# Transposing a third weight matrix in 32x32 squares on VectorE instead of with TensorE, in a two-layer fp32 kernel with NF4 dequantisation

## What is computed

```python
def layer1(x):                     # x: 1024 tokens x 512
    approx_up, delta = x @ up_w.T, x @ gate_w.T - local_point          # 512 -> 128
    out = approx_up @ local_approx_output.T
    for m in range(1, 7):          # powers of |delta| / m!, signed, cut off at 2.5 for m > 4
        out = out + (dterm(delta, m) * approx_up) @ fuse_weight[:, :, m - 1].T
    return out + (silu(x @ ffn_gate_w.T) * (x @ ffn_up_w.T)) @ ffn_down_w.T   # 512 -> 1248 -> 512

def nf4(w):                        # blocks of 64 elements along a row
    absmax = max(|block|)
    return nearest of 16 codes to (block / absmax) * absmax

def layer2(x):                     # w1, w2: 1376 x 512; w3: 512 x 1376
    h = silu(x @ nf4(w1).T) * (x @ nf4(w2).T)
    return h @ nf4(w3).T

x = layernorm(x + layer1(x)); x = layernorm(x + layer2(x))
```

## Time and profile before

| | us |
|---|---|
| three runs, median | 418.53 |
| lowest, highest | 418.44, 418.89 |
| the profiled execution, its own time | 419.06 |
| its span, first to last instruction | 417.2 |
| TensorE's granted clock over the span | 0.994 of full speed |

### The profile page before, as it was taken

How to read it: one execution, slowest core, us unless ns; L and a number is a source line. 1 busy time by engine, 2 the same in 40 slices (tenths; PEclk the granted TensorE clock), 3 DMA queues, 4 the chain that set the end, 5 groups by cost and what they waited for, 6 DMA issues and landing times.

```text
span 417.2 us, 5429 instructions
## 1 busy us (share of the span) xinstructions
PE 408.3 (98%) x1820; PEld 334.0 (80%) x1820; DVE 314.2 (75%) x371; ACT 263.9 (63%) x356; POOL 291.3 (70%) x230
## 2 busy tenths in 40 slices
PE   8999999999999999999999999999999999999992
PEld 6888888888878888788888888888888878888882
DVE  3629879879887978999969989898999874115025
ACT  5476676686877547557864976879867864332612
POOL 0078998888995499917992668999989984444330
PEclk9999999999999999999999999999999999999997
DMA  8993110000004342003042000000000000000202
GB/s 267 395 409 131 52 38 26 27 25 25 27 25 126 102 147 101 26 0 103 0 176 97 2 0 1 2 0 0 3 0 0 2 0 2 1 2 1 101 2 101
DMA packets 9355, 26.50 MB, mean 64 GB/s; under 512 B 1296, under 2 KB 1552, under 8 KB 8816
## 3 DMA queue, kind: packets, MB, share of 16 engines
q1 hardware_dynamic: 9328, 26.16, 17.8%
HBM read 24.06 MB, written 2.10 MB: 63 GB/s over the span
## 4 chain that ended last, share of the span: by engine, by line
PE 91%; POOL 2%; DVE 2%; DMA 2%; issue 1%; ACT 0%; SPq 0%; POOLq 0%
PE PS L1178 30%; PE PS L1180 30%; PE PS L1179 30%; DMA h<-xT 2%; POOL l_lo L1133 1%; PE PS L1291 1%; PE PS L1281 1%; POOL level L1103 1%; DVE stats L889 1%; DVE R L884 0%; ACT R L659 0%; DVE x_lo L970 0%; ACT x_hi L573 0%; DVE mv L898 0%; SPq L537 0%
## 5 line engine op out<-in xcount | busy, mean ns | idle before, releaser
L1103 POOL TENSOR_SCALAR level<-side 128x1024 f32<-128x1024 int8 (+2 forms) x119 | 130.0, 1092 | 29.3 <-DVE PS L812 12.1
L1178 PE MATMUL PS<-x_hi,w_hi 128*128 128x512 f32 (+1 forms) x352 | 137.6, 391 | 0.2 <-DVE x_lo L970 0.2
L1180 PE MATMUL PS<-x_hi,w_lo 128*128 128x512 f32 (+1 forms) x352 | 137.1, 390 | 0.0
L1179 PE MATMUL PS<-x_lo,w_hi 128*128 128x512 f32 (+1 forms) x352 | 137.0, 389 | 0.0
L812 DVE TENSOR_TENSOR PS<-PS,level 128x1024 f32<-128x1024 f32 (+2 forms) x102 | 120.3, 1179 | 21.5 <-POOL level L1103 16.8
L573 ACT ACTIVATE side<-Q 128x1024 int8<-128x1024 f32 (+1 forms) x77 | 76.5, 1031 | 18.6 <-DVE PS L808 9.7
L1133 POOL TENSOR_TENSOR l_lo<-h,l_hi 128x512 fp32r<-128x512 f32 (+1 forms) x42 | 58.3, 1396 | 38.5 <-ACT l_hi L573 38.0
L1178 PEld LDWEIGHTS PS<-x_hi,w_hi 128*128 128x128 f32 (+1 forms) x352 | 65.2, 185 | 15.0 <-issue 0.6
L1180 PEld LDWEIGHTS PS<-x_hi,w_lo 128*128 128x128 f32 (+1 forms) x352 | 65.2, 185 | 14.9
L1179 PEld LDWEIGHTS PS<-x_lo,w_hi 128*128 128x128 f32 (+1 forms) x352 | 65.2, 185 | 14.5
L1178 PE MATMUL PS<-x_hi,l_hi 128*128 128x512 f32 x144 | 56.7, 394 | 0.0
(11 more groups left out here) (77 smaller groups left out, 500.4 us busy)
## 6 DMA issues: line engine op xcount, KB each, us to landing
Q<-w SPq DMA_DIRECT2D x10, 512.0 KB, 13.8
raw<-w_in SPq DMA_DIRECT2D x9, 512.0 KB, 11.4
raw<-w_out SPq DMA_DIRECT2D x14, 256.0 KB, 2.6
raw<-w SPq DMA_DIRECT2D x2, 1376.0 KB, 8.4
R<-xN SPq DMA_DIRECT2D x2, 1024.0 KB, 5.4
out<-R SPq DMA_DIRECT2D x8, 256.0 KB, 2.0
raw<-w_fuse SPq DMA_DIRECT2D x7, 256.0 KB, 2.5
h<-xT SPq DMA_DIRECT2D x3, 512.0 KB, 7.1
```

What stands on the lines that cost most here:

```text
L1103: g.tensor_scalar(level_of(s), side_of(s), LIMITS[k][1], LIMITS[k][0], ALU.min, ALU.max).then_inc(s_level, 1)
L1178: t_.matmul(dst, a_hi, b_hi, start=start, stop=False)
L1179: t_.matmul(dst, a_hi, b_lo, start=False, stop=False)
L1180: return t_.matmul(dst, a_lo, b_hi, start=False, stop=stop)
```

## The change

w3 is laid out by the host in squares, as w1 and w2 are, so that VectorE can transpose it: `turn_w3(c)`, one transpose of 128x512 out of the unit into bank 4 + c % 2. TensorE's transposes of w3 are gone. The six w3 units are now pairs of chunks (1024 columns; the last one chunk, 96x512, in `Q[:, 0]`, the others in `raw`), each loaded by its own transfer; the first five wait for the last use of their slot of `raw`, the sixth for the first `turn_nf4`. In this layout a block of 64 elements of a row is in two halves of 32, that lie on different partitions. VectorE takes maxima of the halves (`maxima_of_w3`, at steps 68, 70, ..., 78, which are 8.4 to 9.6), ScalarE copies each half's maximum to where the other half lies (`bring_partners`, ten small copies, before step 10.2), VectorE takes the greater and the reciprocals of all units at once (`scales_of_w3`, at step 10.3). `up2`, the place of the up products, moves from `Q[:, 0]` to `Q[:, 1]`, and ScalarE's first copy into it waits for the second `turn_nf4`. The table SHARE is new for all three engines.

```diff
-PAIR = 2 * F2
...
-UNITS = C2 + 2 * W3_PARTS
+ROWS3 = D // SQ
+W3_UNITS = (C2 + 1) // 2
+UNITS = C2 + W3_UNITS
 def unit_width(u):
...
-    return UW if is_last_third(u) else 2 * NARROW * BLOCK
+    return D * min(2, C2 - 2 * (u - C2))
 def w3_unit_of(c):
-    return C2 + 2 * min(W3_PARTS - 1, (2 * c + 2) // NARROW) + 1
+    return C2 + c // 2
...
+W3_MAXIMA = {NB * (C2 - 3) + 4 + 2 * k: k for k in range(W3_UNITS)}
+W3_PARTNERS, W3_SCALES = NB * C2 - 6, NB * C2 - 5
...
 SHARE = {
     "scalar": [
-        0, 0, 0, 4, 2, 2, 1, 0, 3, 0, 2, 0, 0, 2, 1, 3, 0, 1, 3, 0, 4, 2, 0, 3, 3, 0, 4, 2, 0, 2, 5, 0, 3, 0,
+        0, 0, 0, 4, 0, 4, 1, 0, 3, 0, 1, 0, 1, 3, 0, 3, 0, 1, 3, 0, 4, 0, 1, 4, 3, 0, 4, 2, 0, 2, 5, 0, 3, 0,
...
-        up2 = Q[:, 0, :].rearrange("p (i n) -> p i n", i=2)
+        w3_last = Q[:, 0, 0:D]
+        amax3, rcp3 = (Q[:, 0, i:i + C2 * ROWS3] for i in (D, D + C2 * ROWS3))
+        up2 = Q[:, 1, :].rearrange("p (i n) -> p i n", i=2)
...
         def w3_bank(c):
-            return 4 + c % W3_BANKS
+            return XT_BANK + c % 2
...
-            wait_split(sp, len(JOBS) - 1)
-            wait_split(sp, VECTOR_LOW[-1])
-            for q in range(2):
-                sp.dma_start(w3_tile(q), w3[q * P:(q + 1) * P, :]).then_inc(s_w3[q], 16)
+            for k in range(W3_UNITS):
+                u = C2 + k
+                if u < UNITS - 1:
+                    wait_split(sp, max(j for j in range(len(JOBS)) if j % RAW_SLOTS == k))
+                else:
+                    sp.wait_ge(s_turn, 1)
+                sp.dma_start(unit_read(u), (w3[:, k * UW:(k + 1) * UW] if u < UNITS - 1 else w3_end)).then_inc(s_w3[k], 16)
...
+            def bring_partners():
+                act.wait_ge(s_max3, W3_UNITS)
...
+                copy(other[a, :, even], own[b, :, even]).then_inc(s_other, 1)
...
             def draw_line(s):
                 u, k = STEPS[s]
+                if s == W3_PARTNERS:
+                    bring_partners()
...
-                act.wait_ge(s_w3tr, c + 1)
+                act.wait_ge(s_w3turn, c + 1)
                 wait_w3_slot(act, c)
-                copy(w_slot(2, ("w3", c), p)[0].rearrange("p (q j r) -> p q r j", q=2, r=2),
-                     PS[0:p, w3_bank(c), :].rearrange("p (q r j) -> p q r j", q=2, r=2)).then_inc(s_whi4, 1)
+                copy(w_slot(2, ("w3", c), p)[0].rearrange("p (i b) -> p i b", i=SQ),
+                     PS[0:p, w3_bank(c), :].rearrange("p (b i) -> p i b", i=SQ)).then_inc(s_whi4, 1)
...
+            def maxima_of_w3(k):
...
+                v.tensor_reduce(unit_scales(amax3, u), by_block(u, unit_read(u)), AX_X, ALU.max,
+                                apply_absolute_value=True).then_inc(s_max3, 1)
+            def scales_of_w3():
+                dve.wait_ge(s_other, 10)
+                v.tensor_tensor(amax3, amax3, rcp3, ALU.max).then_inc(s_max3_all, 1)
...
+            def turn_w3(c):
+                beside()
+                dve.wait_ge(s_dq, quantised(w3_unit_of(c)))
+                dve.wait_ge(s_wlo4, C2 + max(0, c - 1))
+                v.transpose(PS[0:rows(c, F2), w3_bank(c), :], w3_chunk(c)).then_inc(s_w3turn, 1)
...
                     for c in range(2):
+                        turn_w3(c)
+                    for c in range(2):
                         lo_w3(c)
-            for c in range(2, W3_BANKS):
+                        turn_w3(c + 2)
+            for c in range(2, W3_AHEAD):
                 lo_w3(c)
+                turn_w3(c + 2)
...
-            def transpose_w3(c):
-                m = rows(c, F2)
-                pe.wait_ge(s_dq, quantised(w3_unit_of(c) if w3_bank(c) < 6 else UNITS - 1))
-                pe.wait_ge(s_wlo4, C2 + (c - W3_BANKS + 1 if c >= W3_BANKS else 0))
-                for q in range(2):
-                    for r in range(2):
-                        last = t_.transpose(PS[0:m, w3_bank(c), (2 * q + r) * P:(2 * q + r + 1) * P],
-                                            w3_tile(q)[:, r * F2 + c * P:r * F2 + c * P + m], ident[:])
-                last.then_inc(s_w3tr, 1)
```

More of the change, by code:

```diff
@@ L156, in units_ahead @@
     return [u for u in range(UNITS) if max(0, NB * u - ahead) == s]
-SCALE_GROUPS = [range(0, 1)] + [range(u, u + 2) for u in range(1, UNITS, 2)]
+SCALE_GROUPS = [range(0, 1)] + [range(u, u + 2) for u in range(1, C2, 2)]
+W3_MAXIMA = {NB * (C2 - 3) + 4 + 2 * k: k for k in range(W3_UNITS)}
+W3_PARTNERS, W3_SCALES = NB * C2 - 6, NB * C2 - 5
 def adds(s):
@@ L271, in build @@
         l_hi, l_lo = sb("l_hi", [P, L_SLOTS, HALF], F32R), sb("l_lo", [P, L_SLOTS, HALF], F32R)
-        raw = sb("raw", [P, 2 * PAIR])
+        raw = sb("raw", [P, RAW_SLOTS * 1024])
         Q = sb("Q", [P, C2, UW])
@@ L345, in build @@
         s_q = [sem(f"s_q{i}") for i in range(C2)]
-        s_w3 = [sem(f"s_w3_{q}") for q in range(2)]
+        s_w3 = [sem(f"s_w3_{k}") for k in range(W3_UNITS)]
         s_out = sem("s_out")
@@ L453, in w3_bank, with normalised @@
         def w3_bank(c):
-            return 4 + c % W3_BANKS
-        def unit_count(u):
-            return sum(2 if is_last_third(x) else 1 for x in range(u + 1))
+            return XT_BANK + c % 2
         def scaled(u):
[L463 to L468, removed]
+            return [u in group for group in SCALE_GROUPS].index(True) + 1 if u < C2 else len(SCALE_GROUPS) + 1
+        def normalised(u):
+            return u + 1
+        quantised = normalised
         def unit_read(u):
@@ L472, in unit_read, with w3_chunk, by_block, unit_scales @@
                 return Q[:, u, 0:unit_width(u)]
[L473 to L481, removed]
-            if u < C2:
[L483 to L494, removed]
-        def spread(t, u, b, n):
-            v, p = per_block(t, u, b, n), unit_rows(u)
-            if n == 2 * NARROW:
-                return v.unsqueeze(3).broadcast_to([p, 2, NARROW, BLOCK])
-            return v.unsqueeze(2).broadcast_to([p, n, BLOCK])
+            k = u - C2
+            return (w3_last if u == UNITS - 1 else raw[:, k * UW:(k + 1) * UW])[0:unit_rows(u)]
+        def w3_chunk(c):
+            k = c % 2 * D
+            return unit_read(w3_unit_of(c))[:, k:k + D]
+        def by_block(u, tile):
+            return tile.rearrange("p (b e) -> p b e", e=BLOCK if u < C2 else SQ)
+        def unit_scales(t, u):
+            if u < C2:
+                return t[:, (u + 1) % t.shape[1], 0:unit_width(u) // BLOCK]
+            b = (u - C2) * UW // SQ
+            return t[0:unit_rows(u), b:b + unit_width(u) // SQ]
+        def spread(t, t3, u):
+            v = unit_scales(t if u < C2 else t3, u)
+            p, n = v.shape
+            return v.unsqueeze(2).broadcast_to([p, n, BLOCK if u < C2 else SQ])
         def side_of(s):
@@ L573, in copy @@
                 return nc.scalar.activation(dst, src, ACT.Copy, **kw)
+            def bring_partners():
+                act.wait_ge(s_max3, W3_UNITS)
+                own, other = (t.rearrange("p (c b) -> p c b", b=ROWS3) for t in (amax3, rcp3))
+                even, odd = slice(0, ROWS3, 2), slice(1, ROWS3, 2)
+                a, b, c, d = (slice(i * SQ, (i + 1) * SQ) for i in range(4))
+                full = slice(0, C2 - 1)
+                later = slice(1, C2)
+                copy(other[a, :, even], own[b, :, even]).then_inc(s_other, 1)
+                copy(other[b, :, even], own[a, :, even]).then_inc(s_other, 1)
+                copy(other[c, full, even], own[d, full, even]).then_inc(s_other, 1)
+                copy(other[d, full, even], own[c, full, even]).then_inc(s_other, 1)
+                copy(other[b, :, odd], own[c, :, odd]).then_inc(s_other, 1)
+                copy(other[c, :, odd], own[b, :, odd]).then_inc(s_other, 1)
+                copy(other[d, full, odd], own[a, later, odd]).then_inc(s_other, 1)
+                copy(other[a, later, odd], own[d, full, odd]).then_inc(s_other, 1)
+                copy(other[c, C2 - 1, even], own[a, 0, odd]).then_inc(s_other, 1)
+                copy(other[a, 0, odd], own[c, C2 - 1, even]).then_inc(s_other, 1)
             def draw_line(s):
                 u, k = STEPS[s]
+                if s == W3_PARTNERS:
+                    bring_partners()
                 if k == 0:
                     act.wait_ge(s_nrm, normalised(u))
-                    if is_last_third(u):
-                        act.wait_ge(s_dq, quantised(u - 4))
                 if s >= NR:
@@ L1334, in _ @@
                     transpose_x(TILES + 1)
-                elif (f, half) == (C2 - 1, 0):
-                    for c in range(2):
-                        transpose_w3(c)
-            for c in range(2, W3_BANKS):
-                transpose_w3(c)
             for n in range(PASS_START[2], PASS_START[3] - TAILS[2]):
@@ L1382 @@
     fuse = a(L0_attn_fuse_weight)
+    w3_rows = np.zeros((D, C2 * P), np.float32)
+    w3_rows[:, :F2] = a(L0_ffn_w3)[order]
+    w3_rows = w3_rows.reshape(SQ, ROWS3, C2, P // SQ, SQ)
     arrays = {
@@ L1394 @@
         "w12": by_squares(a(L0_ffn_w1), a(L0_ffn_w2)),
```

(4 more changed lines are left out.)

78 lines of the change are left out of this document (36 added, 42 removed), and 24 rows, old and new, of the table SHARE.

## The result

The changed kernel takes **413.5 us** (median of 4 runs, 413.27 to 413.98) where the kernel before takes 418.61 (4 runs, 418.44 to 418.89): a ratio of 0.9878, interval 0.9866 to 0.9889. Predicted were 413.3 us, in a range of 412.6 to 415.8. The profiled execution took 413.98 us and spans 411.8; before it was 417.2, so 5.4 us less.

A forecast was written before the change was run, and what follows sets the result against it. The prediction took TensorE, busy 98% of the span, as the bound. Saving 0.87 + 0.98 + 7 x 0.48 = 5.2 us, with all added work costed at nothing, gave 418.53 - 5.2 = 413.3 us, range 412.6 to 415.8.

The forecast's parts named there:

- The 5.2 us taken off: TensorE's queue: removing the 44 transposes of w3 saves 0.87 + 0.98 + 7 x 0.48 = 5.2 us.
- 7 x 0.48: First pass over w3: seven jobs with four transposes each, every period 0.48 us shorter without them (3.20 to 2.72).
- The 0.87 and 0.98 us: TensorE's chain: cost of two sets of eight transposes, the 0.98 holding some 0.11 us of waiting for the last dequantised unit.
- Rival 3: No gain: the transposes filled time in which TensorE would wait anyway; 418.5 us, chance 0.03.
- What VectorE got: VectorE's added work: eleven transposes at 0.68 us, 7.5 together; low halves 0.69 each; new maximum and reciprocal under 1 us.
- Rival 2: First w3 pass: PSUM reads at a stride of 32 elements are dear, VectorE becomes the bound; 421 to 426.5 us, chance 0.05.
- Is it hidden: First w3 pass: VectorE's new chain costs nothing, with cover of 2.4 us at chunk 2 and about 7 at chunk 10.
- the last pair's banks: TensorE's first w3 job, third tile: ScalarE frees these banks with a margin of only 0.2 to 0.3 us.
- Place (a): Layer 1, input chunk 7: GpSimd's low half ends at 94.7 against 95.0, margin 0.3 us; no wait, up to 1 us.
- Place (b): Boundary of the layers: two w3 maxima on VectorE between products feeding the normalisation; costs nothing, up to 1 us.
- Place (c): GpSimd's queue of low halves until 168.7, same instructions in another order: nothing, 0.5 us either way.
- Rival 1: The new deal leaks: margins of 0.3 us don't hold, costing 0.7 to 3 us; 414.0 to 416.5 us, chance 0.17.

The follow-up runs named there:

- the doubling: The kernel before with every transpose of w3 done twice on TensorE (88 instead of 44): 423.65 us.
- b_none: The kernel before without any transpose of w3 on TensorE, queues and deal of steps otherwise as before (w3 not transposed, time only): 415.53 us.
- a_in7: The changed kernel with one more level ahead of the low half of input chunk 7 on GpSimd: 414.94 us.
- a_early: The changed kernel with VectorE's last eleven steps (7 of ScalarE's, 6 of GpSimd's) put back, VectorE's all ahead of chunk 0's low half: 426.87 us.
- the tripled kernel: The changed kernel with each of VectorE's eleven transposes of w3 done three times: 424.73 us.

## Why the prediction was right

**The bound.** TensorE without a pause, and every other engine free until late: right. Its busy time fell by 5.1 us (408.3 to 403.2), and the other 0.3 of the 5.4 are small waits.

**The 5.2 us taken off.** The number was right and one part of its reason was not. 7 x 0.48 is what the period shows (3.20 to 2.72), and the doubling confirms it. The 0.87 and 0.98 us for the two sets of eight came back too (1.8 us: the first matmul of w3 is 2.0 us earlier, 0.3 of it from before this stage), but not because the transposes had cost that. b_none shows that with them gone TensorE waits 1.66 us at the same place, for a low half that stood behind the last unit. The step that was incomplete is in "What the change removes", where I took them as cost of their own, with only 0.11 us of waiting in them. The fact stood one part further on ("the last unit was written just as TensorE asked for it"); the conclusion, that these 1.85 us come only if the new deal moves that unit out of the way, was not drawn. It did, and the prediction had laid out the new queue and found no wait in it, so the sum held; but these 1.85 us are right by luck as the price of the transposes, for which they were taken. Rival 3 was right in the small: of the 5.2 us some 1.7 lay beside work that TensorE would have had to wait for.

**What VectorE got.** The transposes take 714 ns each (I took 0.68 us), the low halves with their stride of 32 elements 670 (0.69), ScalarE's split 590 (two w_hi of 128x512), less than the 630 of the earlier trace rows and no more than its plain copies out of PSUM of that width (592). Rival 2's premise, a dear read of PSUM at a stride, is false: here it is free. Its counter-argument held for VectorE alone: before, ScalarE's split wrote every second element and took 628 ns (two w_hi), 0.04 us more than a plain copy. Two small terms were under-sized: the scales of all w3 units take 0.33 + 0.76 + 1.25 = 2.35 us where I said under 1. I had left out the middle one, which sets a floor under the maxima. The reciprocal goes with the count (0.35 us for 32 numbers, 1.25 for 176); why the middle one takes 0.76 is not shown, but the same instruction on 32 numbers took from 0.17 to 1.22 us in this execution. The ten copies take 2.6 us where I said about 2. Both stand some 90 us ahead of their use: GpSimd waited 1.5 us for the reciprocals, TensorE for neither.

**Is it hidden.** Yes. VectorE after, in the stretch that was laid out:

```profile
340.86 0.68 DVE L974 TENSOR_TENSOR w_lo<-PS,w_hi 128x512 fp32r<-128x512 f32 x1
...
346.50 0.69 DVE L974 TENSOR_TENSOR x_lo<-PS,x_hi 128x512 fp32r<-128x512 f32 x1 [0.27 <-ACT x_hi L559]
...
363.38 0.67 DVE L974 TENSOR_TENSOR x_lo<-PS,x_hi 128x512 fp32r<-128x512 f32 x1
364.12 0.69 DVE L974 TENSOR_TENSOR w_lo<-PS,w_hi 96x512 fp32r<-96x512 f32 x1
```

Chunk 2 is ready at 347.2 (predicted near 347.6), chunk 10 at 364.8 (near 365). The cover at chunk 2 is 2.4 us, as said, and at chunk 10 6.6; chunk 9, with 4.6, was passed over. At the last pair's banks the margin of 0.2 to 0.3 us was not there: the third tile's first matmul (345.56) took 0.30 us to the next start instead of 0.23. The two evacuations run from 344.39, just behind the end of the pair's last record, to 345.46. The next job's six matmuls had begun at 344.19 already; I had counted them from that end. The margin for ScalarE's own queue was 1.0 us rather than 0.2.

**Place (a).** GpSimd's low half of chunk 7 after, and ScalarE's evacuation of pair 13, which answer to the earlier trace rows:

```profile
92.29 2.41 POOL L1152 TENSOR_TENSOR w_lo<-raw,w_hi 128x1024 fp32r<-128x1024 f32 x1
```
```profile
95.05 0.60 ACT L642 ACTIVATE h<-PS 128x512 f32<-128x512 f32 x1 [1.18 <-PE PS L1210]
```

It ends at 94.70, the predicted 94.7, and TensorE loses under 0.05 us (the pair's first two matmuls start at 94.85 and 95.11). It took 2.41 us, the shorter of the two times in the earlier trace rows.

**Place (b).** No wait; between 214.2 and 217 TensorE even comes 0.17 us further ahead of the kernel before, and what had held it there is not shown. VectorE reaches the first maximum at 213.75 (predicted 213.9) and its data are there (a transfer of 512 KB landed 3.9 us after its issue, median of five); the last low half of x is there 0.3 us sooner than before:

```profile
213.75 1.18 DVE L805 TENSOR_REDUCE Q<-raw 128x32 f32<-128x1024 f32 x1
...
233.52 1.29 DVE L937 TENSOR_TENSOR x_lo<-PS,x_hi 128x512 fp32r<-128x512 f32 x2 [0.74 <-ACT x_hi L559]
```

**Place (c).** Up to 0.2 us gained rather than nothing: behind the matmul at 168.29 TensorE stood still for 0.35 us before, behind that at 168.38 for 0.19 after. It is inside the 0.5 us allowed.

**Rival 1** (leaks) did not happen, though a_in7 shows that one more step of 1.1 us at (a) would have given it. Its chance of 0.17 was not too high: of three margins called small, that at (a) was, that at the banks was gone by 0.07 us while ScalarE's own was misread, and (b) was put to no test of its own.

## What to carry to other kernels

Work that stands in the bottleneck's queue just ahead of a late operand is free as long as the operand is late: removing it pays only if what it waited beside is moved as well, so ask of each piece removed when the next operand is ready without it. And when a step is dealt to another engine, look at which needed result stands behind it in that engine's queue; two steps of 3.8 us, moved behind two low halves of 1.3 in all, decided a third of this change. A pause of the bottleneck can cost more than its length, through the clock, as in a_early and in the tripled kernel.
